# A routed-expert layer: row norms, transposes, gate products and low parts issued in another order

## What is computed

```python
qkv = x @ w_qkv                                   # x: (8, 512, 128)
q_proj = _elu1(jnp.einsum('bhnd,hdf->bhnf', q, proj_matrix))   # 16 heads of 8 features, 32 out
k_proj = _elu1(jnp.einsum('bhnd,hdf->bhnf', k, proj_matrix))
kv = jnp.einsum('bhnf,bhnd->bhfd', k_proj, v)
attn = jnp.einsum('bhnf,bhfd->bhnd', q_proj, kv)
z = 1.0 / (jnp.einsum('bhnf,bhf->bhn', q_proj, k_proj.sum(axis=2)) + 1e-08)
x = _layernorm(x + (attn * z[..., None] -> tokens) @ w_out + b_out)
gate_scores = jnp.einsum('bsd,ed->bse', _l2norm(x @ Wp.T), _l2norm(sim_matrix)) / temperature
top_v, top_i = jax.lax.top_k(gate_scores, 2)      # softmax of the two gives the weights
out = sum over the two experts e of  p_e * (gelu(x @ W1[e] + b1[e]) @ W2[e] + b2[e])
x = _layernorm(x + out)
```

## Time and profile before

| | value |
|---|---|
| median of three executions | 309.04 us (306.79 to 310.75) |
| profiled execution, its own time and its span | 311.13 us, 309.3 us |
| TensorE products busy | 281.7 us, 91% of the span, 2,548 |
| TensorE weight loads busy | 255.4 us, 83% |
| VectorE busy | 214.4 us, 69% |
| ScalarE busy | 190.2 us, 61% |
| GpSimd busy | 174.5 us, 56% |
| mean granted TensorE clock | 0.963 of 2.4 GHz |

### The profile page before, as it was taken

One profiled execution on the slowest core, in us unless ns is written; L12 is line 12 of the kernel. 1 busy time (PEld: TensorE's weight loads), 2 busy tenths in 40 slices (PEclk: granted clock), 3 DMA queues, 4 the chain that ended last, 5 costly groups with the idle time before them and its releaser, 6 DMA issues.

```text
span 309.3 us, 8850 instructions
## 1 busy us (share of the span) xinstructions
PE 281.7 (91%) x2548; PEld 255.4 (83%) x2548; DVE 214.4 (69%) x828; ACT 190.2 (61%) x511; POOL 174.5 (56%) x200
## 2 busy tenths in 40 slices
PE   8999999999999999989999999999999999999500
PEld 7778887878787787867999899999999999999500
DVE  1865969696978999686565766554445588888770
ACT  4686667585656667546556455555565666888642
POOL 2300216656566666656435777777777547767730
PEclk9999999999999999989799999999999999999955
DMA  5990101021011112331101133333421744553140
GB/s 139 344 293 19 37 3 60 28 74 34 28 61 37 36 35 74 82 90 47 33 17 38 46 103 95 95 98 106 114 71 54 222 133 149 171 173 118 49 170 35
DMA packets 23557, 27.93 MB, mean 90 GB/s; under 512 B 4250, under 2 KB 16584, under 8 KB 23510
## 3 DMA queue, kind: packets, MB, share of 16 engines
q1 hardware_dynamic: 19190, 18.82, 21.2%
q0 software_dynamic: 4320, 8.53, 8.2%
HBM read 16.17 MB, written 11.62 MB: 90 GB/s over the span
## 4 chain that ended last, share of the span: by engine, by line
PE 32%; DVE 12%; issue 5%; DVEq 3%; POOL 2%; ACT 1%; POOLq 0%; ACTq 0%
PE pair L641 13%; PE pair L661 6%; PE bank L661 6%; DVEq L1098 3%; DVE w_t L1104 2%; DVE z L1273 2%; DVE z L1267 2%; PE pair L630 2%; DVE st L1279 1%; PE bank L563 1%; POOL rs L373 1%; PE bank L589 1%; DVE y_sb L1256 1%; DVE xtT L1092 1%; POOL expert_rows L407 1%
## 5 line engine op out<-in xcount | busy, mean ns | idle before, releaser
L885 ACT ACTIVATE h<-pair,w_t 128x128 f32<-128x128 f32 x284 | 81.0, 369 | 52.3 <-PE pair L641 52.3
L384 POOL DMA_INDIRECT routed_rows<-x,slot_of x64 | 66.3, 1035 | 45.3 <-issue 38.5
L407 POOL DMA_INDIRECT expert_rows<-y_sb,xt x71 | 71.6, 1009 | 30.8 <-issue 16.0
L641 PE MATMUL pair<-xtT,w_t 128*128 128x128 f32 x568 | 76.5, 278 | 1.1 <-DVE w_t L1104 1.1
L641 PEld LDWEIGHTS pair<-xtT,w_t 128*128 128x128 f32 x568 | 69.9, 194 | 2.1 <-DVE w_t L1104 1.9
L1104 DVE COPY w_t<-w_sb 128x516 f32 x71 | 31.9, 452 | 24.5 <-issue 23.3
L803 ACT ACTIVATE expo<-pair 128x1024 f32<-128x1024 f32 x32 | 32.8, 1026 | 18.3 <-PE pair L496 16.9
L661 PE MATMUL pair<-w_sb,h 128*128 x288 | 38.9, 279 | 0.4 <-ACT h L885 0.4
L661 PE MATMUL bank<-w_sb,h 128*128 x280 | 37.1, 275 | 0.0
L661 PEld LDWEIGHTS pair<-w_sb,h 128*128 128x128 f32 x288 | 35.6, 195 | 0.6 <-issue 0.6
L661 PEld LDWEIGHTS bank<-w_sb,h 128*128 128x128 f32 x280 | 34.3, 193 | 0.0
(11 more groups left out here) (193 smaller groups left out, 472.0 us busy)
## 6 DMA issues: line engine op xcount, KB each, us to landing
xt<-routed_rows SPq DMA_DIRECT2D x71, 66.0 KB, 2.0
yb<-expert_rows SPq DMA_DIRECT2D x7, 512.0 KB
x_tok<-in_L_attn_x_dram SPq DMA_DIRECT2D x8, 256.0 KB, 2.9
w_sb<-in_L_ffn_W_dram SPq DMA_DIRECT2D x1, 2048.0 KB, 9.6
out_dram<-z SPq DMA_DIRECT2D x7, 256.0 KB, 3.0
expert_rows<-y_sb,xt POOLq DMA_INDIRECT x71, 2.3
routed_rows<-x,slot_of POOLq DMA_INDIRECT x64, 2.4
routed_rows<-pad_rows SPq DMA_DIRECT2D x8, 66.0 KB
```

The costliest lines, as they stand in the source:

```text
L384: pool.indirect_dma_start(out=xs_dram, out_offset=bass.IndirectOffsetOnAxis(ap=slot_of[:, s, t, k:k + 1], axis=0), in_=x2[:, s * T + t, :] ...
L407: pool.indirect_dma_start(out=y_dram, out_offset=bass.IndirectOffsetOnAxis(ap=xt_u[:, i % XR, D:D + 1], axis=0), in_=y_sb[:, i % YR, :], i ...
L641: mm = nc.tensor.matmul(B[i % 2][:, cols(c)], w1_t[:, i % WR, cols(c)], xtT[:, i % 2, :], start=True, stop=True)
L885: ins = nc.scalar.activation(h[:, i % 2, cols(c)], B[i % 2][:, cols(c)], ACT.Gelu, bias=w1_t[:, i % WR, F + c:F + c + 1])
```

## The change

No instruction is added, removed or resized; the numbers of instructions are those of before on every engine. Five things move:

1. VectorE: the four row norms of sequence `r` go ahead of the mask of sequence `s`'s sums, and the low part of x goes from the front of both to behind them.
2. TensorE: the transposes of the normed rows go ahead of the transposed sums and of `keys(s+1, 0, 0)`, right behind `values(s+1)`.
3. TensorE: the gate's products go ahead of `keys(s, 0, 1)` and of its wait.
4. TensorE: the transposes of the next x go ahead of the mix with the output weights.
5. ScalarE: the copy of the transposed rows goes ahead of the copy of the sums.

The title under which the change was made also speaks of sums in two full passes; the diff holds nothing of that kind, and both kernels have it.

```diff
--- before.py
+++ after.py
@@ -712,15 +712,15 @@
 
             for s in range(1, SEQS):
                 r, q = s - 1, s - 2
-
-                pe.wait_ge(s_kv_bd, s)
-                keys(s, 0, 1)
                 if q >= 0:
                     if s == 2:
                         pe.wait_ge(s_gw, 2)
                     gate(q, 0)
                     gate(q, 1)
-                else:
+
+                pe.wait_ge(s_kv_bd, s)
+                keys(s, 0, 1)
+                if q < 0:
                     fold_gate()
 
                     pe.wait_ge(s_gw, 1)
@@ -737,9 +737,9 @@
                 else:
                     pe.wait_ge(s_gw, 2)
                 transpose_attn(r)
-                mix_heads(r)
                 if s + 1 < SEQS:
                     transpose_x(s + 1)
+                mix_heads(r)
                 queries(s, 1, 0)
                 queries(s, 1, 1)
                 sum_keys_values(s, 0)
@@ -751,10 +751,10 @@
                     up(0)
                 if s + 1 < SEQS:
                     values(s + 1)
+                transpose_x2(r)
                 transpose_sums(s)
                 if s + 1 < SEQS:
                     keys(s + 1, 0, 0)
-                transpose_x2(r)
 
             for i in range(2, NT + 2):
                 at = PE_TAIL.get(i)
@@ -857,9 +857,9 @@
 
             for s in range(1, SEQS):
                 r, q = s - 1, s - 2
-                take_sums(r)
                 if q >= 0:
                     take_x2(q)
+                take_sums(r)
                 if q >= 0:
                     square_norms(q)
                 exps(s, 0)
@@ -874,8 +874,8 @@
                 if s + 1 < SEQS:
                     take_x(s + 1)
                 exps(s, 3)
+            take_x2(SEQS - 2)
             take_sums(SEQS - 1)
-            take_x2(SEQS - 2)
             load_table(ACT.Gelu)
 
             def gelu(i):
@@ -1234,12 +1234,12 @@
                     weigh(q)
                 sum_and_statistics(r)
                 features(s, 2)
+                if s == SEQS - 1:
+                    take_tile(0)
+                norm_rows(r)
+                mask_key_values(s)
                 if s + 1 < SEQS:
                     x_low(s + 1)
-                if s == SEQS - 1:
-                    take_tile(0)
-                mask_key_values(s)
-                norm_rows(r)
                 if s == SEQS - 1:
                     take_tile(1)
                 features(s, 3)
```

## The result

The changed kernel takes 312.04 us (median of 11 executions, 311.73 to 313.69), the kernel before 308.93 us beside it on the same chip (306.78 to 310.75). The ratio is 1.0123, with a 95% interval of 1.0085 to 1.016: slower by 1.2%. The forecast was 317.0 us and +2.6%; the time lies within the range of 311.5 to 322, but half of the forecast loss did not come.

The account below looks back on a forecast made before the run. TensorE was taken to bound the kernel, loop delays reaching the end one for one. Passes 6.0, pass 7 -1.3 and clock 3.3 gave +8.0 on the profiled 311.13 us: 319.1, or 317.0 against the median; range 311.5 to 322.

Parts of the forecast that it names:

- Root held, row norms wait: GpSimd's statistics root ends 0.90 us behind VectorE's features, so row norms moved ahead gain nothing and VectorE idles 0.9 us.
- The root not held: Rival: the root ends 1.05 us after its start, each pass loses 0.6 us instead of 1.0; 311.5 us, chance 0.08.
- the root there at once: Rival: the rows' input is ready when the features end, so a pass costs nothing; 306.1 us, chance 0.07.
- Cost of a pass: First numerators on TensorE come 1.0 us later in each of six passes: 6.0 us (4.8 to 7.2).
- The walk on the clock: One profiled pass retimed part by part under the new order, putting the first numerators at 92.5 instead of 91.50.
- the 0.3 us forecast ahead of them: TensorE's first keys would wait another 0.3 us for VectorE's low part, now behind row norms and mask.
- Gate ahead of the second keys: On TensorE the gate's 0.92 us goes between two 0.70 us key steps; its own 0.43 us wait goes.
- cover for the edit on x: x's transposes ahead of TensorE's mix start queries 0.44 us earlier, absorbed by the wait for the rows: worth nothing.
- Pass 7: Last pass of the loop: gate's root ahead of the features (-0.9) and no rows' wait for a mask (-0.4), together -1.3 us.
- The other term, 0.4 us: In pass 7 the rows no longer wait for a mask, so TensorE's loader loses its 0.4 us wait: -0.4.
- The clock, +3.3 us: New TensorE waits in six passes bring two more falls to half clock, 1.65 us each.
- no more falls: Rival: the clock falls no more often, or once less; only +4.7 or +3.0 us left, 313.7 or 312.1 us; chance 0.2.

Follow-up runs that it names:

- the kernel with x ahead: Kernel before with only the transposes of the next x moved ahead of the mix; 308.05 us, ratio 1.0007.
- the kernel with the low part late: Changed kernel with GpSimd's statistics root ahead of the third scatter, VectorE ordered row norms, mask, low part, third features; 331.24 us, ratio 1.0755.
- the kernel with two fills: Changed kernel with two unused fills of a spare tile on VectorE ahead of the row norms; 327.42 us, ratio 1.0624.
- the kernel with the transposes back: Changed kernel with the rows' transposes back behind the first keys on TensorE, VectorE's new order and the gate's new place kept; 330.36 us.

## Why the prediction was off

**What bounds the kernel, and where the loss comes from: right.** Passes got longer, and every microsecond of it arrived at the end: the tail from the last root on differs by less than 0.2 us.

**Root held, row norms wait: right.** Forecast were 0.9 us idle and a root ending 0.90 us behind the features; measured 0.94 and 0.89. The root not held and the root there at once (the last two rivals) fell, the latter also when it was made real.

**Cost of a pass: right in kind, 0.2 too high.** Forecast +1.0, measured +0.82. The walk on the clock placed the mask 1.21 us behind the start of the row norms and the low part 1.54; they start 1.04 and 1.37 behind it (90.83 and 91.16 against 89.79). The row's 1.29 us are not free of overlap: what follows starts 0.25 us before their recorded end, where I had taken off 0.08 as between the features' neighbours. So the first keys do not wait for the low part, and the 0.3 us forecast ahead of them are not there. Over six passes this is 1.1 us too much.

**Gate ahead of the second keys, with no price of its own: right only in this sum.** As one of the walk's terms it disappeared in the order of the products. Without the edits on the rows it costs 0.70 us in a pass, and with them nothing that was seen (18.24 us with it, 18.40 with it undone). The prediction named its cover for the edit on x, but not for this one; the cover of the second keys was the copy of the rows.

**Pass 7: the size right, one of its two terms for a wrong reason.** The gate's root was not held, and its pass got shorter by 0.30 where 0.81 was due to be added: 1.1 us for a forecast of 0.9. The other term, 0.4 us because the rows would no longer wait for the mask, was a misreading. In the kernel with x ahead, which has the old order and no fall in pass 7, the rows' transposes stand 2.82 us behind the root, and 2.80 in the changed kernel; the 3.89 of before came with the fall, which ended just ahead of that root and left TensorE behind. The 0.88 us that this stretch gained are the fall that is not there: with the old order and without it the stretch takes 20.78 us instead of 21.85.

**The clock, +3.3 us: this is the step that failed.** Two more falls of 1.65 us were taken, "the size of what fell"; none came. The waits of pass 7 (0.47, 0.67 and 0.37 us) were taken as a measure for one wait of 1.5 and one of 0.3. The fifteen passes without a fall at 1.31 us show that the comparison did not hold, and the five of six with one at 2.2 us that the idea behind it, longer waits bring falls, did. The three waits were no safe sign of a fall even where they came from: the kernel with x ahead has 0.46, 0.67 and 0.37 us in its pass 7, and no fall there. A second error is in the same step: a fall was treated as a property of the profiled execution of before, when it is one of a third of its runs. The step from that execution to the median, 2.1 us, holds this fall, and the changed kernel had nothing of it to lose.

Together, on the profiled executions: forecast +8.0, measured +2.4. Of the difference of 5.6 us, 3.3 is the clock, 1.1 the passes, 0.7 pass 7 and what follows it (with the 0.88 us of the fall that is not there), and 0.5 the head, the tail and what lies around the spans of the two executions. The rival "no more falls", at 0.2, had 313.7 or 312.1 us, and that is what came: 312.0 in the best clock group, 313.6 in the other. Part of this match is luck: its +4.7 is the same 6.0 - 1.3 as in the forecast, and on the traces these two terms measured +4.9 and -1.1, so +3.8.

## What to carry to other kernels

Where one engine waits for a result in two stages (made, then copied), list the pieces of its own work that can stand under each wait, and move none out: one uncovered piece costs about its whole length (0.70 us a pass here), a second one hardly more (0.81 for both). So the costs of edits to one such place don't add, and each should be priced in the order that the others leave. Cutting the hand-over into halves shortens both waits without touching the order; here that gained half a per cent, where no reordering gained anything.

A clock fall seen in one profiled execution is to be counted only after asking in how many of the timed runs it is: groups in the times, with the mean clock beside them, show it before any experiment.

And an engine that works in order, like GpSimd here, passes every delay on: before heavy VectorE steps are put back to back, look at which of its instructions will start beside them.

## What the runs showed of the hardware that was not expected

- A scatter of GpSimd (an indirect DMA's issue, about 1.0 us) that starts beside feature steps of VectorE ends 0.84 to 0.92 us behind them: 1.50 to 1.61 us beside one step in the kernel before, 2.99 us beside two, 3.61 us in the kernel with the low part late, where low part and features follow one another. The roots end 0.89 to 0.91 us behind such a step.
- The low part on VectorE (two inputs in SBUF, 0.69 us) holds a root that starts beside it: 1.42 or 1.43 us in the six passes of one kernel that have a low part, 1.04 in its seventh, which has none, and 1.04 or 1.05 in all seven of another kernel that differs only in the low part's place.
- A wait of TensorE of 1.31 to 1.38 us in this place was followed by no fall of the granted clock in 15 passes, one of 2.18 to 2.24 us by a fall of some 3.3 us in 5 of 6, and each of six of 4.6 to 4.8 us came with a fall, of 3.3 us once and 6.8 us five times. One of 1.76 us, in pass 7 of the kernel with two fills, was followed by none in the next 6 us. With two waits close together (1.5 and 0.67 us) the clock fell in some passes and not in others, in one and the same execution. Why one fall in the kernel with the transposes back lasted 24 us stays open.
